# A graph kernel's block pipeline behind layer 0: degree roots ahead of the loop, and the store of the normalised rows moved to a later pass

## The reference

```python
x = _layernorm(x + _L0_gnn_ref(x, src, dst, edge_weight, W), axis=-1)     # weighted sum over edges, @ W.T
x = _layernorm(x + _L1_gnn_ref(x, edge_index, W1, b1, ..., Wfc, bfc), axis=-1)
x = _layernorm(x + _L2_gnn_ref(x, src, dst, edge_weight, eps, w1, b1, w2, b2), axis=-1)
x = _layernorm(x + _L3_gnn_ref(x, edge_index, W, b, gamma, beta), axis=-1)
```

```python
deg = segment_sum(ones, d)                    # in-degree, self loop included
dinv = rsqrt(max(deg, 1))
out = segment_sum((x @ W)[s] * (dinv[s] * dinv[d])[:, None], d) + b
...
cat = concatenate([x, x1, x2], axis=1)        # x1, x2: both convolutions, batch-normed, relu
return relu(cat @ Wfc + bfc)
```

## Time and profile before

| | |
|---|---|
| median of three runs | 3458.49 us (3456.47 to 3461.07) |
| profiled execution, its own time | 3460.09 us |
| its span, first to last instruction | 3458.8 us, mean granted clock 0.907 |
| busy share PE / PEld / DVE / ACT / POOL | 82 / 61 / 57 / 37 / 71% |
| block pipeline (1270 to 1418 us) | 148 us |
| second pass of layer 1, its blocks beside (1836 to 2078 us) | about 242 us |

### The profile page before, as it was taken

One profiled execution on the slowest core, in us unless ns is written; L12 is line 12 of the kernel. 1 busy time (PEld: TensorE's weight loads), 2 busy tenths in 40 slices (PEclk: granted clock), 3 DMA queues, 4 the chain that ended last, 5 costly groups with the idle time before them and its releaser, 6 DMA issues. The chain is left out here.

```text
span 3458.8 us, 60258 instructions
## 1 busy us (share of the span) xinstructions
PE 2842.7 (82%) x19203; PEld 2100.9 (61%) x19220; DVE 1983.2 (57%) x6763; ACT 1275.6 (37%) x3485; POOL 2462.4 (71%) x2238
## 2 busy tenths in 40 slices
PE   5989877878888859789977997778888875699995
PEld 4777655656666648444446774366666764466664
DVE  7889777777787729442243434443444564245557
ACT  5566666776877739200010002500111232001123
POOL 3888777786676667577747776777777774777773
PEclk8999998999999979899978997589999998799996
DMA  8787788888888879678856886755556564988884
GB/s 273 112 147 113 142 154 148 155 155 170 179 175 170 180 175 354 180 213 231 237 141 177 226 224 172 217 172 158 162 176 181 159 178 124 297 235 247 252 251 137
DMA packets 658436, 652.79 MB, mean 189 GB/s; under 512 B 87902, under 2 KB 606476, under 8 KB 656588
## 3 DMA queue, kind: packets, MB, share of 16 engines
q0 software_dynamic: 153600, 258.41, 37.3%
q1 hardware_dynamic: 430670, 331.83, 31.2%
q10 hardware_dynamic: 73854, 58.70, 5.4%
HBM read 434.19 MB, written 214.52 MB: 188 GB/s over the span
## 5 line engine op out<-in xcount | busy, mean ns | idle before, releaser
L1701 POOL DMA_INDIRECT A<-rows_buf,big x572 | 902.4, 1578 | 333.8 <-issue 143.5
L882 POOL DMA_INDIRECT rows_buf<-T,idx x888 | 847.7, 955 | 275.9 <-issue 272.2
L976 PE MATMUL PSA<-S,rows_buf 128*128 128x128 bf16 (+2 forms) x5904 | 582.5, 254 | 213.9 <-DMA rows_buf<-X,idx 103.5
L976 PEld LDWEIGHTS PSA<-S,rows_buf 128*128 128x128 bf16 (+2 forms) x5904 | 523.3, 142 | 296.8 <-DMA rows_buf<-X,idx 88.0
L882 POOL DMA_INDIRECT rows_buf<-X,idx x528 | 509.5, 965 | 160.9 <-issue 157.8
L1032 DVE TENSOR_TENSOR accT<-PSA,accT 128x256 f32 (+2 forms) x354 | 132.8, 375 | 835.7 <-PE PSA L976 828.5
L1556 DVE TENSOR_TENSOR accT<-PSA,accT 128x392 f32 (+5 forms) x366 | 239.7, 655 | 173.0 <-issue 59.6
L1394 PE MATMUL PSA<-XRS,rows_buf 128*128 128x256 f32 x1144 | 313.0, 398 | 6.4 <-ACT rows_buf L1406 6.4
L793 ACT ACTIVATE accT<-accT,vec 128x500 f32<-128x500 f32 (+3 forms) x26 | 17.7, 693 | 666.5 <-DVE accT L791 666.4
L1406 ACT ACTIVATE rows_buf<-PSA 128x512 f32<-128x512 f32 x286 | 168.0, 593 | 186.1 <-PE PSA L1394 175.8
L1394 PEld LDWEIGHTS PSA<-XRS,rows_buf 128*128 128x128 f32 x1144 | 209.8, 197 | 32.0 <-ACT rows_buf L1385 6.8
(11 more groups left out here) (315 smaller groups left out, 5805.3 us busy)
## 6 DMA issues: line engine op xcount, KB each, us to landing
XRS<-Ad SPq DMA_DIRECT2D x400, 256.0 KB
Ad<-accT SPq DMA_DIRECT2D x224, 196.0 KB
XRS<-in_xpad SPq DMA_DIRECT2D x192, 128.0 KB, 3.3
Awd<-accT SPq DMA_DIRECT2D x48, 392.0 KB, 3.6
A<-accT SPq DMA_DIRECT2D x9, 1600.0 KB
rows_buf<-T,idx POOLq DMA_INDIRECT x888
rows_buf<-A SPq DMA_DIRECT2D x24, 512.0 KB
accT<-A SPq DMA_DIRECT2D x24, 512.0 KB, 6.1
```

Source lines behind the costliest of these rows:

```text
L882: s_hg[slot(i)][j // 2].on(pool.indirect_dma_start(Gv(slot(i), j), None, table, bass.IndirectOffsetOnAxis(idx[:, c:c + 1], 0)), 16)
L976: last = pe.matmul(PS[bank_of(i)][0:F, W * h:W * h + W], Gv(slot(i), j)[:, o:o + F], hits[:, i % SRING, j, :], start=j + part == 0, stop=j ...
L1701: s_k[n].on(pool.indirect_dma_start(A, bass.IndirectOffsetOnAxis(tgt[:, c:c + 1], 0), G[:, i % RING, j, :], None, compute_op=ALU.add), 16)
```

## The change

Two edits. First, the 49 degree matmuls, the roots and the reciprocals leave the pipeline: `degree_inverses()` is called once before it. It issues all 49 matmuls into one bank, then two roots and two reciprocals (48 blocks at once and the last). Second, the store of X1 leaves the pipeline. Instead `product_beside` in layer 1's second pass transposes the block's two halves of xT back (`pe.transpose`, L2203 in the new file), ACT copies them out of PSUM (L2215) and stores them from its queue (L2217). In `product_beside` PE now waits for ACT's copy of the block before (s_ca) where it waited for DVE's addition (s_pb); a ring slot of normalised rows is free for DVE when PE has transposed it, where it was free when it had been stored.

```diff
@@ turn_sums, sums_out
         for h in range(2):
-            pe.transpose(PS[t % 2][...], part_sums[slot][...], ident[0:r, 0:r])
-        s_ta.mark(t, pe.matmul(PS[t % 2][0:r, 256:257], degB[0:1, cols(t)], ones[0:1, 0:1], start=True, stop=True))
+            ins = pe.transpose(PS[t % 2][...], part_sums[slot][...], ident[0:r, 0:r])
+        s_ta.mark(t, ins)
...
-        s_nq.mark(t, sc.activation(dnm[0:rows(t), t:t + 1], PS[t % 2][0:rows(t), 256:257], ACT.Sqrt))
...
-    def degree_inverses(t):
-        s_nq.of(v, t)
-        s_dr.mark(t, v.reciprocal(dnm[0:rows(t), t:t + 1], dnm[0:rows(t), t:t + 1]))
+    def degree_inverses():
+        for t in range(NT):
+            ins = pe.matmul(PS[7][0:rows(t), t:t + 1], degB[0:1, cols(t)], ones[0:1, 0:1], start=True, stop=True)
+        s_dq.on(ins)
+        s_dq.by(sc)
+        r = rows(NT - 1)
+        sc.activation(dnm[:, 0:NT - 1], PS[7][:, 0:NT - 1], ACT.Sqrt)
+        s_nq.on(sc.activation(dnm[0:r, NT - 1:NT], PS[7][0:r, NT - 1:NT], ACT.Sqrt))
+        s_nq.by(v)
+        v.reciprocal(dnm[:, 0:NT - 1], dnm[:, 0:NT - 1])
+        s_dr.on(v.reciprocal(dnm[0:r, NT - 1:NT], dnm[0:r, NT - 1:NT]))
@@ add_residual
-            free(ring, t)
+            if t >= ring:
+                s_tp.of(v, t - ring)
@@ the pipeline's call
+    degree_inverses()
-             + [(14, store(ZR0, X1)), (14, transpose(...)), (15, turned(xT))]
+             + [(14, transpose(...)), (15, turned(xT))]
@@ product_beside
+    PX = weights[:, 256:768].rearrange("p (r d) -> p r d", d=D)
...
         if t:
-            s_pb.of(pe, t - 1)
+            s_ca.of(pe, t - 1)
+        for h in range(2):
+            pe.transpose(PS[7][0:r, D + 128 * h:D + 128 * h + 128], xT[:, h, cols(t)], ident[:, :])
...
         s_st[t % 3].mark(t, sc.dma_start(X2[cols(t), :], PB[0:r, t % 3, :]), 16)
+        if t >= 2:
+            s_ts[t % 2].of(sc, t - 2)
+        s_ca.mark(t, sc.activation(PX[0:r, t % 2, :], PS[7][0:r, D:2 * D], ACT.Identity))
+        s_ca.of(sc, t)
+        s_ts[t % 2].mark(t, sc.dma_start(X1[cols(t), :], PX[0:r, t % 2, :]), 16)
```

More of the change, by code:

```diff
@@ L1981, in turn_sums @@
         for h in range(2):
-            pe.transpose(PS[t % 2][:, 128 * h:128 * h + r], part_sums[slot][0:r, 0, 128 * h:128 * h + 128], ident[0:r, 0:r])
-        s_ta.mark(t, pe.matmul(PS[t % 2][0:r, 256:257], degB[0:1, cols(t)], ones[0:1, 0:1], start=True, stop=True))
+            ins = pe.transpose(PS[t % 2][:, 128 * h:128 * h + r], part_sums[slot][0:r, 0, 128 * h:128 * h + 128], ident[0:r, 0:r])
+        s_ta.mark(t, ins)
     def sums_out(t):
@@ L1989, in sums_out @@
             s_mm.of(sc, t - 4)
-        s_nq.mark(t, sc.activation(dnm[0:rows(t), t:t + 1], PS[t % 2][0:rows(t), 256:257], ACT.Sqrt))
         s_ca.mark(t, sc.activation(sumT[:, t % 4, :, 0:rows(t)], p, ACT.Identity))
-    def degree_inverses(t):
-        s_nq.of(v, t)
-        s_dr.mark(t, v.reciprocal(dnm[0:rows(t), t:t + 1], dnm[0:rows(t), t:t + 1]))
+    def degree_inverses():
[9 more added lines that the diff above has]
+        s_dr.on(v.reciprocal(dnm[0:r, NT - 1:NT], dnm[0:r, NT - 1:NT]))
     def spread_degrees(t):
-        s_dr.of(pe, t)
+        if t == 0:
+            s_dr.by(pe)
         s_ca.of(pe, min(t + 1, NT - 1))
@@ L2061, in rounds_from @@
         start_rounds()
-    pipeline([(0, load_sums), (2, add_pairs), (3, add_last), (4, turn_sums), (5, sums_out), (6, degree_inverses), (7, spread_degrees), (8, degrees_out), (4, residual(a["xpad"])),
+    degree_inverses()
+    pipeline([(0, load_sums), (2, add_pairs), (3, add_last), (4, turn_sums), (5, sums_out), (7, spread_degrees), (8, degrees_out), (4, residual(a["xpad"])),
               (6, multiply(lambda t: [(sumT[:, t % 4, h, 0:rows(t)], W0[:, h, :]) for h in range(2)], lambda t: s_ca.of(pe, t))),
@@ L2066, in build @@
              + normalise(8, ZR0, 0, s_z, s_nm)
-             + [(14, store(ZR0, X1)), (14, transpose(lambda t: zs(ZR0, t), s_nm)), (15, turned(xT))]
-             + table_rows(16, T1, 128, lambda i, t: xT[:, i, cols(t)], [W1[:, 0, :], W1[:, 1, :]], lambda t: (s_tc.of(pe, t), s_dr.of(sc, t)), queue=sc))
+             + [(14, transpose(lambda t: zs(ZR0, t), s_nm)), (15, turned(xT))]
+             + table_rows(16, T1, 128, lambda i, t: xT[:, i, cols(t)], [W1[:, 0, :], W1[:, 1, :]], lambda t: (s_tc.of(pe, t), s_dr.by(sc)), queue=sc))
     s_do.by(v)
```

## The result

The changed kernel took 3470.65 us (median of 6 runs, 3466.68 to 3474.48), the kernel before 3457.55 us on the same chip (6 runs, 3450.79 to 3461.49): a ratio of 1.0034 [1.0023, 1.0045]. A second comparison, made beside later runs, gave 3468.59 against 3455.51 us, 1.0034 [1.0021, 1.0046]. So the change costs 12 to 13 us; "the same" at 3456 us was wrong, and the time lies outside the range.

What follows compares the result with a forecast made beforehand. PE and the DMA engines were both taken as full in the block pipeline. Start +7, loop -9.3, last load -0.8, drain -0.3 and second pass +1 sum to -2.4 us: 3456 us, range 3446 to 3467.

Steps and rivals of the forecast that it cites:

- the second pass was sized at +1: Layer 1's second pass: the added transposes, copy and store cost +1 us, bounds 0 and 10.8.
- One costs 0.31 us ... I take 15.2.: Pipeline start: 49 degree matmuls take 15.2 us, from choices 10.8, 15.2 and 25.0; first transposes come 11.4 us late.
- The 2.4 us from the run to the first transposes: Pipeline start: 2.4 us from the last degree matmul through roots, reciprocals and first addition to the first transposes.
- Part of that is won back ... I keep +7.: First blocks: PE's shorter blocks win back 5.6 of 11.4 us late; +7 us kept at the 16th block.
- the bound of 16: Pipeline start: upper bound of the delay kept at the 16th block, 16 us, if the degree matmuls take 25 us.
- 2.06, with 2.01 and 2.20 as the ends ... -9.3.: Steady pipeline: 31 blocks go from 2.36 to 2.06 us each, saving 9.3 us, ends -10.9 and -5.0.
- three bounds (PE, bytes, ACT): Steady pipeline, per block: PE 2.05 us or less, DMA bytes 2.01, ACT below 2.07.
- DVE's 2.09 from the early stretch: Early pipeline: six blocks took 2.09 us each with most of DVE's work, taken as evidence against DVE setting the pace.
- another engine takes over: Rival, steady pipeline: DVE needs 2.2 us or more per block beside POOL, loop gives -5 or nothing; 3462 us, 10%.
- The last load, -0.8.: Pipeline end: the last block's load is issued behind less queued work, saving 0.8 us; most of its wait stays.
- both bad ends at once: Range 3446 to 3467 us holds both ends of start and loop, but not a dear start together with a slow loop.
- the second rival's, 3466 us: Rival, pipeline start: degree matmuls cost their low-clock 0.51 us each, 25.0 in all, +16 at the start; 3466 us, 10%.

Runs made afterwards that it cites:

- The batches: Both edits, but the degree matmuls in seven batches of seven inside the pipeline, against the kernel before: 0.9990 on one chip, 3449.97 us and 0.9988 on another.
- the kernels without the long run: Kernels that do not issue 49 degree matmuls ahead of the pipeline, such as both edits with seven batches of seven: 3449.97 us, 0.9988 against the kernel before.
- the kernel with batches and XR at step 5: Both edits, degree matmuls in seven batches of seven, load of residual x one step later (5 for 4), against the kernel before: 3448.71 us, 0.9983.
- the second profile: The changed kernel run again as it is, beside the later runs, against the kernel before: 3468.59 us, 1.0034; pipeline length 160.60 us.
- XR at step 4: The load of residual x left at its original pipeline step, as in the changed kernel, 3470.65 us, 1.0034 against the kernel before.

## Why the prediction was wrong

- **Where the change matters.** Right in this: both edits matter only in the pipeline, and the second pass was sized at +1 with nothing of it found (0.9999).
- **"One costs 0.31 us ... I take 15.2."** This is the first step that failed. A matmul of the run costs 0.428 us, 20.96 in all, because the granted clock stayed at 0.50 over it. I had the row that said so (clock 0.50 until 1286, 0.51 us for one there) and set a price of the high clock against it. The batches show 0.44 and 0.23 at the two levels, so the single matmuls of the rows, 0.51 and 0.31, were each some 0.08 dearer than one in a run; why is not shown. The 2.4 us from the run to the first transposes were 2.62. Those came 1290.86 - 1267.54 = 23.3 us behind the first load, against 6.2 before: 17.1 late in place of 11.4.
- **"Part of that is won back ... I keep +7."** This failed by more. From the addition of block 8 to that of block 16 it took 17.24 us before (1288.49 to 1305.73) and 17.48 after. From block 10 on the additions do come faster, 1.88 us apart, but with POOL waiting 0.6 for DMA each time: the loads set that pace, not PE's spare time. And what this wins was lost by the first loads after the standstill (blocks 8 to 10: 6.24 us in place of 4.51). The DMA engines had moved nothing for 11 us and did not make that up. The prediction named this standstill, and the clock, and raised 11.4 - 5.6 = 5.8 to 7 for both. Kept at block 16: +13.7 and +13.0, near the bound of 16, which I had given only to the dearest price of the matmuls. In the kernels without the long run block 16's addition comes 33.5 to 35.6 us behind the first load, against 35.37 before.
- **"2.06, with 2.01 and 2.20 as the ends ... -9.3."** This step failed too. None of the three bounds (PE, bytes, ACT) was the one that held: 2.18 and 2.33 came out, -5.6 and -0.9 us. DVE's 2.09 from the early stretch was no proof: L762, which takes DVE 0.28 to 1.36 us per block, begins only at 1309.19, behind that stretch. In the changed kernel DVE is busy 66.19 of 67.62 us and 71.12 of 72.32, and PE waits for its L2024. Halving POOL's addition, in the kernel with batches and XR at step 5, brought 2.01. So what holds the loop once PE and the DMA engines are relieved is, by that run, the path over POOL's addition and DVE, with DVE standing still beside POOL as a likely part of it. That comes near the rival "another engine takes over", to which I gave 10%. That the order of SP's loads has a share in it is not shown.
- **The last load, -0.8.** The addition of block 48 came 9.97 and 11.41 us behind that of block 47, in place of 10.32: nothing is gained, and splitting the load took 5.6 us off the length. By the Trainium skill (DMA: Bandwidth & Descriptors, Why a DMA increments its semaphore by 16 and not by 1) a transfer goes on the greatest number of engines up to 16 that divides its slowest dimension: two for 106 rows, 16 for 96. The runs fit that, 14.05 us against 7.3 for the same rows as 96 + 10; how many engines a load used no view here shows.
- **The range.** It left out "both bad ends at once". They came together: the start near its dear end and the loop near or beyond its own, 13.0 - 0.9 + 1.1 - 0.2 = +13.0 in the second profile, and 3457.55 + 13.0 = 3470.6 is what was measured. The nearest forecast was the second rival's, 3466 us: it had the start nearly right and gave the loop its whole gain.

Open: in the kernel before, PE and the DMA engines each seem to hold the loop at about the same pace, but in the run with the first edit alone SP also stands 34.4 us ahead of the store of X1, waiting for ACT, and no run takes that wait away alone. With both edits the five profiles with XR at step 4 lie between 2.18 and 2.38. Why the changed kernel's loop takes 67.6 us in one profile and 72.3 in another is open too. Taking 0.15, 0.28 and 0.40 us as the unstretched L668, L762 and L1974, these lines take 24 us more than that in the faster profile and 29 in the slower; that fits the 4.7 us between them, but what brings DVE and POOL together more often is not known.

## What to carry to other kernels

Work pulled ahead of a pipeline isn't paid by what it costs in steady state: price it at the clock of the place, and add the standstill of the loads behind full slots, which spare time of PE behind it did not give back here. Made in small batches inside the pipeline, the same work cost nothing that shows. Before a loop is given the gain of a relieved engine, look for stretched instructions (a mean far above the shortest of the same shape) on the engines that are next in line. In the kernel before they cost next to nothing, as other engines set the pace; once these were relieved, they were the likely takers of the gain. A last block with fewer rows is worth a look at its landing time.

## What the runs showed of the hardware

- A one-row fp32 matmul (two passes) back to back: 0.43 to 0.44 us at granted clock 0.50, 0.23 at 1.00. 98 passes in a row over 20.96 us, PE busy without a gap, all ran at 0.50.
- A DVE instruction of one column (L668) or of two fp32 operands (L1974) that met a POOL tensor_tensor of 512 columns took 1.22 and 1.38 us in the lines above, in place of 0.15 and 0.41, and PE waited 1.25 us for DVE behind it. L1974, L762 and L668 appear thus stretched, while L649 and L2024 (L2014 before), of which the second reads PSUM, show 0.38 to 0.43 every time. How many are stretched differs between profiles of one and the same pipeline: 31 over 0.6 us in one, 10 in another, none of these over 0.65.
- A load of 424 KB in 106 rows took 13.3 to 16.0 us from issue to addition in all the kernels that had it, beside 4 to 9 for 512 KB in 128 rows; as 96 + 10 rows it took 7.3 and 7.5.
- The same program took 3455 us on one chip and 3835 on another, at a pipeline length that differed little: one and the same kernel (the batches) 146.2 and 148.5 us.
